# Attention and a gated low-rank layer, 16 sequences on one core: the low-rank products moved beside the second scores on TensorE, and the order of sums, maxima and residuals changed on VectorE

## What is computed

```
h  = layernorm(x)
q, k, v = h Wq + bq, h Wk + bk, h Wv + bv        # 2 heads of 64
q, k: the last 32 features of each head rotated by the position
a  = softmax(q k^T / 8) v ;  a = a Wo + bo
x  = x + layernorm(a)
h  = layernorm(x)
base   = h W^T
proj   = (h Wp^T + bp) / |h Wp^T + bp|            # 32 features
lw     = softmax(proj sim_n * scale) over 4 experts; only the largest is kept
res    = sum_e lw_e * (h Wd_e^T) Wu_e^T           # ranks 1, 2, 4, 8: 15 in all
x  = x + layernorm(base + res)
```

## Time and profile before

| | |
|---|---|
| time, median of 3 | 164.67 us |
| the profiled execution's own time | 165.49 us |
| its span | 163.7 us |
| TensorE busy (products) | 132.5 us, 81% |
| VectorE busy | 128.4 us, 78% |
| ScalarE busy | 111.2 us, 68% |
| GpSimd busy | 89.8 us, 55% |
| TensorE's granted clock | full but for slices 6 and 7 of the page's 40 (about 20 to 27 us) and the last six (from about 143 us), which are at half |

### The profile page before, as it was taken

One profiled execution on the slowest core, in us unless ns is written; L12 is line 12 of the kernel. 1 busy time (PEld: TensorE's weight loads), 2 busy tenths in 40 slices (PEclk: granted clock), 3 DMA queues, 4 the chain that ended last, 5 costly groups with the idle time before them and its releaser, 6 DMA issues.

```text
span 163.7 us, 3006 instructions
## 1 busy us (share of the span) xinstructions
PE 132.5 (81%) x865; PEld 106.9 (65%) x865; DVE 128.4 (78%) x540; ACT 111.2 (68%) x369; POOL 89.8 (55%) x148
## 2 busy tenths in 40 slices
PE   0467579988989999999999999999999699166040
PEld 0246257877779778887987888798788589135010
DVE  3569966586798999999989998898797798754602
ACT  3157545883979699789969997996997767240130
POOL 4281960580566595867767685875569506405201
PEclk9999956999999999999999999999999999955555
DMA  3524230000000000200020010001001000001001
GB/s 100 185 72 122 70 122 0 4 2 0 2 0 4 2 0 0 68 0 0 2 68 2 0 64 4 0 0 64 2 6 64 0 4 34 30 0 64 0 0 64
DMA packets 4911, 5.02 MB, mean 31 GB/s; under 512 B 369, under 2 KB 4640, under 8 KB 4896
## 3 DMA queue, kind: packets, MB, share of 16 engines
q1 hardware_dynamic: 4512, 4.46, 8.5%
q10 hardware_dynamic: 384, 0.38, 0.7%
HBM read 2.74 MB, written 2.10 MB: 30 GB/s over the span
## 4 chain that ended last, share of the span: by engine, by line
PE 71%; DVE 13%; ACT 6%; POOL 3%; DMA 3%; issue 2%; POOLq 1%; DVEq 0%; ACTq 0%
PE ps_s L838 11%; PE ps_a L858 8%; PE ps_z L879 7%; PE ps_b L858 5%; PE ps_c L858 4%; PE ps_a L848 4%; PE ps_z L892 4%; PE ps_b L812 3%; DMA x_all<-x 3%; PE ps_b L848 3%; PE ps_c L828 2%; PE ps_s L869 2%; PE ps_c L848 2%; PE ps_s L828 2%; PE ps_d L819 2%
## 5 line engine op out<-in xcount | busy, mean ns | idle before, releaser
L320 ACT ACTIVATE probs<-ps_s,neg_max 128x256 f32<-128x256 f32 x64 | 27.1, 489 | 11.8 <-DVE neg_max L474 11.8
L474 DVE TENSOR_REDUCE neg_max<-ps_s 128x2 f32<-128x512 f32 x32 | 21.7, 683 | 4.6 <-PE ps_s L838 4.6
L838 PE MATMUL ps_s<-qk_t 64*128 64x256 f32 x128 | 19.2, 418 | 0.9 <-ACT probs L320 0.9
L858 PE MATMUL ps_a<-v_all,probs_t 128*128 128x129 f32 x128 | 17.6, 280 | 0.0
L858 PEld LDWEIGHTS ps_a<-v_all,probs_t 128*128 128x128 f32 x128 | 15.6, 191 | 2.3 <-issue 2.3
L216 POOL TENSOR_TENSOR turn<-qk,sin_x 128x256 f32<-128x256 f32 x16 | 11.7, 733 | 9.4 <-ACT qk L304 9.0
L879 PE MATMUL ps_z<-w_z,x_t 128*128 128x190 f32 x64 | 13.9, 352 | 2.2 <-DVE x_all L589 2.2
L838 PEld LDWEIGHTS ps_s<-qk_t 64*128 64x128 f32 x128 | 11.9, 195 | 5.8 <-issue 5.2
L589 DVE SCALAR_TENSOR_TENSOR x_all<-ps_z,rsz,x_all 128x128 f32<-128x128 f32 x32 | 9.3, 345 | 7.6 <-POOL rsz L237 7.6
L227 POOL TENSOR_TENSOR inv_norm<-norm,power 128x4 f32<-128x4 f32 x8 | 8.1, 1014 | 13.0 <-DVE norm L543 13.0
L231 POOL TENSOR_TENSOR rsy<-var_y,power 128x4 f32<-128x4 f32 x8 | 8.6, 1071 | 11.5 <-ACT sq_y L331 11.5
(11 more groups left out here) (198 smaller groups left out, 403.6 us busy)
## 6 DMA issues: line engine op xcount, KB each, us to landing
x_all<-x SPq DMA_DIRECT2D x8, 256.0 KB, 2.7
out<-x_all SPq DMA_DIRECT2D x7, 256.0 KB, 2.1
vec<-vectors ACTq DMA_DIRECT2D x1, 273.0 KB, 4.3
w_raw<-w_attn SPq DMA_DIRECT2D x1, 256.0 KB, 5.1
out<-x_all SPq DMA_DIRECT2D x2, 128.0 KB, 1.7
ffn_raw<-w_ffn ACTq DMA_DIRECT2D x1, 71.5 KB
down_raw<-w_down ACTq DMA_DIRECT2D x1, 23.5 KB
sim_raw<-sim ACTq DMA_DIRECT2D x1, 0.5 KB
```

Of the source, the lines that this page charges most:

```text
L320: last = act.activation(probs[:, u, j, :], ps_s[u % 2][:, j * T:(j + 1) * T], ACT.Exp, bias=neg_max[:, u, j:j + 1])
L474: dve.tensor_reduce(neg_max[:, u, :], ps_s[u % 2][:, :].rearrange("p (j k) -> p j k", j=TILES), AX.X, ALU.max, negate=True).then_inc(max_r ...
L838: last = pe.matmul(ps_s[h][:, j * T:(j + 1) * T], qk_t[r, b, 0, j * P:(j + 1) * P], qk_t[r, b, 1, :], start=True, stop=True)
L858: last = pe.matmul(unit_bank[u][:, j * VW:(j + 1) * VW], probs_t[:, u, i, j * P:(j + 1) * P], v_all[:, at:at + VW], start=(i == 0), stop=( ...
```

## The change

On TensorE, weigh(a, 0) moves ahead of turn_probs(a, 1), and scores(a, 1) moves behind turn_gated(a-2), directly ahead of low_rank(a-2). On VectorE, weights_sum and both add_heads of unit 0 move up behind the gates, ahead of mean and variance of pair a+3; row_max(a, 3) follows row_max(a, 2) directly; the residuals 1 to 3 and the statistics of pair a-1 come behind both. No instruction is added or removed, and no semaphore count changes.

```diff
@@ VectorE, pass a @@
                 if done:
                     gates(a - 2)
+                if now:
+                    weights_sum(a, 0)
+                    add_head(a, 0, 0)
+                    add_head(a, 0, 1)
                 if has(a + 3):
                     mean(a + 3)
                     variance(a + 3)
                 if now:
                     row_max(a, 2)
+                    row_max(a, 3)
+                if a == 0:
+                    later_weights(2)
                 if last_:
                     residual_y(a - 1, 1)
                     residual_y(a - 1, 2)
-                if now:
-                    row_max(a, 3)
-                    weights_sum(a, 0)
-                if a == 0:
-                    later_weights(2)
-                if last_:
+                    residual_y(a - 1, 3)
                     stats_2(a - 1, 0)
-                if now:
-                    add_head(a, 0, 0)
-                if last_:
                     stats_2(a - 1, 1)
-                if now:
-                    add_head(a, 0, 1)
-                if last_:
-                    residual_y(a - 1, 3)
                     stats_2(a - 1, 2)
                     stats_2(a - 1, 3)
@@ TensorE, pass a @@
                 if nxt:
                     project_qkv(a + 1, 2, (qkt_out, 2 * a + 2) if now else (xt_low, 1))
                 if now:
-                    scores(a, 1, (probs_ready, 4 * a + 2))
+                    weigh(a, 0)
                     turn_probs(a, 1, (v_out, 4 * (a + 1) + 1) if nxt else (y_ready, 4 * (a - 1) + 2))
                 if a == 0:
                     later_weights(1)
                 if done:
                     turn_gated(a - 2, ...)
                 if now:
-                    weigh(a, 0)
+                    scores(a, 1, (probs_ready, 4 * a + 2))
                 if done:
                     low_rank(a - 2)
```

## The result

The changed kernel takes 172.97 us (median of 4 runs, 171.62 to 174.24) against 164.94 for the kernel before in the same session: 1.046 times, 95% interval 1.038 to 1.054. A later session gave 173.08 against 165.38, 1.047 (1.043 to 1.052). By the two medians it is 8.0 us slower; one of the four runs (174.24) was in a slower state, and the ratio, which leaves it out, gives 7.6 (172.6 and 165.0 on average). The forecast was 6.2 us more, 170.9, with 167.3 to 173.4 as the range.

What follows compares the result with a forecast made beforehand. A full TensorE queue was taken to bound the 14.6 us steady pass; 2.7 (passes 2 to 4) + 0.6 + 0.5 + 1.4 + 0.7 + 0.3 = 6.2 us on the 164.67 median gave 170.9 us, range 167.3 to 173.4.

Steps and rivals of the forecast that it cites:

- The saved switches: TensorE, passes 2 to 7: two groups of 64-row products become one, saving 0.34 us of dead time per pass.
- weigh 0 waits for the copy: TensorE: weigh 0 must wait for ScalarE's 0.62 us copy of the turned probabilities, exposing 0.3 + 0.1 us.
- ScalarE stops at exps 2: ScalarE idles 1.05 us ahead of exps 2 for row_max 2, because the scores are done 1.85 us later.
- The port: VectorE: mean and variance, held by GpSimd's rope, delay row_max 2 by 0.32 us; bounds 0 and 0.6.
- The ring's way back: Chain ScalarE, VectorE, ScalarE, from exps 3 over rows_up to next exps 0, bounds passes, 0.6 us longer than TensorE's.
- the idle ahead of exps 0: ScalarE's idle 1.20 us ahead of exps 0 was to pay for the rest of the 1.05 and 0.5 us delays.
- Pass 0: First pass: later row_max 2 and exps delay turn_probs 3, +0.7 us; bounds 0.4 and 1.4.
- Pass 7: Last pass, without projections to hide waits: turn_probs 3 comes 1.4 us later; bounds 1.0 and 1.7.
- gaps of 1 us are few: The prediction's reason, beside full speed in the steady pass, against a drop of the clock within the passes.
- the rival of harder hold-ups: VectorE's mean and variance each held by a rope product, pass 0 at its upper bound: +8 to +9, 173 us; chance 0.16.

Runs made afterwards that it cites:

- the low-rank products apart: Changed kernel with low_rank moved behind weigh 1, making two groups of 64-row products again: 172.19 us against 165.56 for the kernel before, ratio 1.045.
- statistics first: Changed kernel with mean and variance of pair a+3 put back ahead of y of unit 0: 170.77 us against 164.44 for the kernel before, ratio 1.035.
- variance_z first: Changed kernel with ScalarE's variance_z ahead of exps 2 instead of behind them: 169.92 us against 165.56 for the kernel before, ratio 1.030.
- the changed kernel again: The changed kernel measured once more, nothing altered: 173.08 us (6 runs) against 165.38 for the kernel before, ratio 1.047.
- VectorE's part alone: Kernel before with only VectorE's part of the change, TensorE's order as before: 175.44 us against 164.44, ratio 1.067.
- TensorE's part alone: Kernel before with only TensorE's part of the change, VectorE's order as before: 172.92 us against 164.44, ratio 1.050.
- pass 7 as before: Changed kernel with the old order on both engines in pass 7 only: 170.64 us against 164.44 for the kernel before, ratio 1.035.

## Why the prediction was right

- **The saved switches**, 0.34 us per pass: there in the timeline, off the bound, worth nothing in passes 2 to 4. Shown there by the low-rank products apart.
- **weigh 0 waits for the copy**: it starts 0.04 us after ScalarE's 0.61; scores start within 0.01 us of the forecast. Right.
- **ScalarE stops at exps 2**: 1.05 plus 0.32 was forecast. Less the 3.23 us by which the pass lies later, exps 2 start at 91.81; forecast with the port 91.80. turn_probs 3 stands at 94.47 instead of 93.67, +0.8, as 0.5 and 0.3 add up to. Right.
- **The port**: 0.33 for 0.32, removed by statistics first.
- **The ring's way back** was told wrong; that its length came out right was luck. I led it over ScalarE's rows_up. The trace leads it over TensorE: turn_probs 3 late, so project_z late, so VectorE's route (L526) waits 0.45 for it, and rows_low, behind it in the list, with it. Nor did the idle ahead of exps 0 pay for anything. Both ways happen to be nearly equally long here, which is why the size held: 0.6 without statistics (measured 0.60 and 0.59), 0.9 with them (0.86).
- **Pass 0**: 0.7 forecast, 1.29 in the first profile and 14.66 - 14.13 = 0.53 in the second of the changed kernel. Its length follows the early half-speed stretch, which ends 2.2 us behind row_max 0 in the first (28.0), 0.5 in the second (26.3) and 1.4 before (27.1). The kernel with variance_z first has the same program in pass 0 and its stretch ends 1.3 us behind (27.1): 15.02, so at nearly the same clock the order costs 0.9.
- **Pass 7**: 1.4 forecast and 1.40 measured, where the clock stays up (statistics first, the changed kernel again).

The term that was mis-sized is the clock, which the sum put at nothing. I put a drop within the passes aside with "gaps of 1 us are few". In pass 7 the forecast itself had TensorE wait from 129.8 to 131.2 and I didn't ask what the clock would make of it. That is 1.6 us, in those of the runs where it falls there. Between the two first profiles the spans differ by 8.3 us (163.7 and 172.0), 2.1 more than the forecast 6.2: 1.6 from pass 7, some 0.4 from the clock in pass 0 and 0.2 from the order there, the rest 0.1 less than forecast. Nothing of the order's own cost was off by more than 0.2 us per pass.

So the order's cost was forecast rightly, and the whole time came out at 173, where the rival of harder hold-ups stood. That rival's own mechanism failed (0.33 us per pass, not 0.6); its added clause, a drop of the clock within the passes, is what happened. The range reached up to that rival and so held the measured time; the central 170.9 was 2.1 us under it.

## What to carry to other kernels

What is moved back on a full engine delays its readers, less whatever they would have waited or lain ready anyway: here 1.85 us at the scores became 0.86 at the pass. Follow the moved work's results through the fixed order of the next engine before counting what the move saves. Dead time saved is worth something only if that engine is still the bound afterwards. And where an in-order engine waits ahead of a product that another engine needs, ask what lies finished behind it, as in VectorE's part alone.

## What the runs showed of the hardware

- Six of the eleven profiles have a stretch of 3.4 us at half clock within the passes. Two lie in pass 7 (137.2 to 140.6 in the changed kernel, 136.8 to 140.2 with TensorE's part alone) and begin 0.7 and 0.3 us after TensorE had waited 1.44 and 1.43 us for the copy. Four lie around the start of pass 1 (39.0 to 42.5, 38.5 to 41.9, 36.8 to 40.2, 40.0 to 43.4: VectorE's part alone, statistics first, pass 7 as before, the changed kernel again) and begin 1.0 to 2.0 us after a wait of 1.36 or 1.37 us for sim_r at the end of pass 0. Waits of the same length stand about as often without a fall behind them: 1.36 us for sim_r in three profiles (the first of the changed kernel among them), 1.44 us for the copy in four (the second among them). What decides between the two is not shown. One such stretch cost 1.6 us where a profile without it can be set beside it (pass 7: 9.87 and 8.25; pass 1: 16.55 and 14.92).
- A VectorE instruction on four numbers takes 0.65 to 0.69 us instead of 0.16 when it starts within 0.1 us behind the start of one of rope's products, and 0.48 when it starts 0.26 us inside one: it lasts until the product ends. One that reads the scores' bank (row_max, 0.68) was not longer there. GpSimd's power on four numbers (L200, 87.72 to 88.72 in the kernel before) held nothing: a residual that started at 88.04 took its usual 0.34 us.
